# Layer-norm statistics of four token tiles at once, and a first stage that begins with the first four tiles, in an attention and FFN layer on eight cores

## The reference

```python
Q, K, V = x @ wq.T, x @ wk.T, x @ wv.T            # 64 columns each
energy = K.T @ V                                  # 64 x 64, over all tokens
x = layernorm(x + (Q @ energy) * sqrt(3/64) @ wo.T)
h = silu((x @ w1.T) * s1) * ((x @ w2.T) * s2)      # 4096 wide
h = gelu((h @ h1.T) * sh1)                         # 4096 x 4096
h = gelu((h @ h2.T) * sh2)                         # 4096 x 4096
x = layernorm(x + (h @ w3.T) * s3)
```

## Time and profile before

| | us |
|---|---|
| median of 3 runs (lowest, highest) | 2842.74 (2729.49, 3065.65) |
| profiled execution, its own time | 2728.27 |
| its span, slowest core (5) | 2726.4 |
| spans of the eight cores | 2723.3 to 2726.4 |
| TensorE, VectorE, ScalarE busy | 2576.0, 712.3, 342.7 |

### The profile page before, as it was taken

The page is one execution under the profiler, slowest core; times in us unless marked ns, Lnnn a source line. Parts: engine busy times, 40 slices in busy tenths (PEclk is TensorE's granted clock), DMA queues, the critical chain, the costliest instruction groups (busy, mean ns, idle before and its releaser), DMA issues.

```text
span 2726.4 us, 30051 instructions; the slowest of 8 cores (2723.3 to 2726.4 us)
## 1 busy us (share of the span) xinstructions
PE 2576.0 (94%) x12610; PEld 1218.3 (45%) x12610; DVE 712.3 (26%) x771; ACT 342.7 (13%) x429; POOL 0.7 (0%) x7
## 2 busy tenths in 40 slices
PE   4553999999999999999999999999999999999998
PEld 3552444444444444444444444444444444444443
DVE  2335333211111222222224433211111111111124
ACT  1103221100000011111101221100000000000001
POOL 0000000000000000000000000000000000000000
PEclk8665999999999999999999999999999999999999
DMA  9996444444444444544473544444444444444453
GB/s 310 340 342 234 156 155 155 156 152 155 154 155 154 146 163 170 179 162 169 166 266 120 190 155 155 156 153 154 155 154 153 150 149 151 153 155 155 154 185 108
DMA packets 65155, 473.34 MB, mean 174 GB/s; under 512 B 7232, under 2 KB 7360, under 8 KB 15872
## 3 DMA queue, kind: packets, MB, share of 16 engines
q1 hardware_dynamic: 56960, 442.07, 46.5%
q10 hardware_dynamic: 8064, 29.36, 3.2%
HBM read 454.62 MB, written 16.78 MB: 173 GB/s over the span
## 4 chain that ended last, share of the span: by engine, by line
PE 89%; DMA 7%; DVE 2%; ACT 1%; issue 1%; SPq 0%; DVEq 0%; ACTq 0%
PE P L283 65%; PE P L248 16%; DMA HB<-xg 7%; PE P L315 4%; PE P L302 4%; DVE GB L585 1%; DVE GB L531 0%; ACT TS L377 0%; DVE X1B L523 0%; PE P L209 0%; DVE P L546 0%; DVE XZ L549 0%; PE P L216 0%; DVE WR L504 0%; PE P L330 0%
## 5 line engine op out<-in xcount | busy, mean ns | idle before, releaser
L283 PE MATMUL P<-GB,WR 128*128 128x512 bf16 x4096 | 887.1, 379 | 0.0
L283 PE MATMUL P<-HB,WR 128*128 128x512 bf16 x4096 | 884.4, 379 | 0.0
L504 DVE CAST WR<-WST 128x2048 bf16<-128x2048 f32 x328 | 401.6, 1225 | 1405.7 <-PE P L283 1405.7
L283 PEld LDWEIGHTS P<-HB,WR 128*128 128x128 bf16 x4096 | 400.8, 98 | 483.3
L283 PEld LDWEIGHTS P<-GB,WR 128*128 128x128 bf16 x4096 | 399.8, 98 | 482.9 <-issue 3.4
L248 PE MATMUL P<-X1T,WR 128*128 128x512 bf16 x2048 | 444.6, 380 | 0.6 <-DVE HB L559 0.6
L248 PEld LDWEIGHTS P<-X1T,WR 128*128 128x128 bf16 x2048 | 200.8, 98 | 243.8 <-issue 3.8
L330 PE MATMUL P<-GB 128*128 128x128 bf16 x1024 | 99.3, 285 | 101.7 <-DVE GB L585 101.7
L438 ACT ACTIVATE GB<-P,SC 128x1024 bf16<-128x1024 f32 x64 | 71.3, 1115 | 784.8 <-PE P L283 784.8
L559 DVE SCALAR_TENSOR_TENSOR HB<-P,SC,TS 128x512 bf16<-128x512 f32 x128 | 96.0, 751 | 273.8 <-ACT TS L425 273.8
L438 ACT ACTIVATE HB<-P,SC 128x1024 bf16<-128x1024 f32 x64 | 71.3, 1115 | 702.5 <-PE P L283 702.4
(11 more groups left out here) (52 smaller groups left out, 345.6 us busy)
## 6 DMA issues: line engine op xcount, KB each, us to landing
WST<-h SPq DMA_DIRECT2D x256, 1024.0 KB, 4.9
WST<-w SPq DMA_DIRECT2D x96, 1024.0 KB, 5.3
HB<-xg SPq DMA_DIRECT2D x32, 2048.0 KB, 22.3
XZ<-x1s ACTq DMA_DIRECT2D x16, 512.0 KB, 4.1
y<-XZ ACTq DMA_DIRECT2D x16, 512.0 KB, 2.9
GB<-xn SPq DMA_DIRECT2D x8, 512.0 KB, 26.9
x1s<-GB ACTq DMA_DIRECT2D x8, 512.0 KB, 2.8
XZ<-xn ACTq DMA_DIRECT2D x8, 512.0 KB, 6.0
```

The source lines that it names most:

```text
L283: mm = t.matmul(ps[:, g * 512:(g + 1) * 512], W[:, j * 128:(j + 1) * 128], src[:, ic * HALF + g * 512:ic * HALF + g * 512 + 512], start=(i ...
L504: v.tensor_copy(dst, wst(n)).then_inc(s_cast, 1)
```

## The change

- **Last group of x.** Group 31 is loaded by four DMAs of 512 KB, each with a semaphore of its own, and cast in four pieces. TensorE takes two of the eight chunks of E for all four token tiles, as each piece is cast.
- **Statistics.** Tiles 0 to 3, then 4 to 7: VectorE does four adds, and MM, VAR, SD, RS and NMR are made for four columns at once. The add of tile 4 stands between VAR and RS of the first four. The 40 one-column instructions become 10 of four columns.
- **Applies.** The bf16 result goes to GB (x1p), a buffer for each tile. VectorE applies tiles 0 to 2 and 4 to 6, ScalarE tiles 3 and 7 (Identity with scale and bias by token). The transposes go in the order 0, 3, 1, 2, then 4, 7, 5, 6.
- **Stage 1.** Parts 0 to 3 of half 0 use chunks 0 to 3 with tiles 0 to 3, parts 4 to 7 the same chunks with tiles 4 to 7. Part 0 waits for four adds and four copies. The transposes of tiles 4 and 7 stand behind part 2, those of 5 and 6 behind part 3, and part 4 waits for all eight copies. The casts of chunks 3 to 6 are moved to the multiplies of parts 0, 4, 5 and 6.
- **The f32 apply** of the eight tiles is on ScalarE (Identity, in place), behind the Silus of parts 8, 10 to 22, each followed by its store to x1s.
- **SP's order** behind xnat 3: chunk 0, xnat 4, 5, chunk 1, xnat 6, 7, chunk 2.

The diff, cut to its core:

```diff
+FIRST = [(m % 4, m // 4) for m in range(8)]
+TURNS = (0, 3, 1, 2, 4, 7, 5, 6)
...
+    def x1p(t):
+        return GB[:, t * E:(t + 1) * E]
...
+    def stage1_part(h, m):
+        return FIRST[m] if h == 0 and m < 8 else (m // 2, m % 2)
...
             def load_x(g):
                 if g >= 4:
                     s_.wait_ge(s_xc, g - 3)
-                s_.dma_start(out=xst(g), in_=xg[g]).then_inc(s_xl[g % 4], 16)
+                if g < NG - 1:
+                    s_.dma_start(out=xst(g), in_=xg[g]).then_inc(s_xl[g % 4], 16)
+                else:
+                    for i in range(4):
+                        s_.dma_start(out=xst(g)[:, i * 1024:(i + 1) * 1024],
+                                     in_=xg[g][:, i * 1024:(i + 1) * 1024]).then_inc(s_xe[i], 16)
...
@@ -191,12 +209,12 @@
             for t in range(4):
                 load_xnat(t)
             load_chunk(0)
-            load_chunk(1)
             load_xnat(4)
             load_xnat(5)
-            load_chunk(2)
+            load_chunk(1)
             load_xnat(6)
             load_xnat(7)
+            load_chunk(2)
             for n in range(NS, 2 * PER_HALF):
                 load_chunk(n)
...
+            def turn_first(j):
+                k = TURNS[j]
+                if j >= 2:
+                    t.wait_ge(s_te, j - 1)
+                if k % 4 == 3:
+                    t.wait_ge(s_x1c, k // 4 + 1)
+                else:
+                    t.wait_ge(s_x1b, 3 * (k // 4) + k % 4 + 1)
+                for c in range(EC):
+                    tp = t.transpose(pt(j % 2)[:, c * 128:(c + 1) * 128],
+                                     x1p(k)[:, c * 128:(c + 1) * 128], IDB[:])
+                tp.then_inc(s_tp, 1)
...
             def stage1(h):
                 for m in range(64):
-                    oc, g = m // 2, m % 2
+                    oc, g = stage1_part(h, m)
                     M = 64 * h + m
                     n = PER_HALF * h + oc
                     if g == 0:
                         t.wait_ge(s_cast, n + 1)
                     if m >= 3:
                         t.wait_ge(s_hv, M - 2)
-                    elif h == 0:
-                        t.wait_ge(s_sum, 8)
                     else:
-                        t.wait_ge(s_sum, (21, 23, 24)[m])
-                    if m < 2:
-                        t.wait_ge(s_te, 8 * h + 4 * (g + 1))
+                        t.wait_ge(s_sum, ((4, 7, 8), (21, 23, 24))[h][m])
+                    if m == 0:
+                        t.wait_ge(s_te, 4 + 12 * h)
+                    if m == 4 and h == 0:
+                        t.wait_ge(s_te, 8)
                     W = wr(RING_HALF * h + oc)
                     ps = pair(h, m)
                     for w in range(2):
@@ -250,6 +281,9 @@
                                           X1T[:, c * HALF + g * 512:c * HALF + g * 512 + 512],
                                           start=(c == 0), stop=(c == EC - 1))
                     mm.then_inc(s_m1, 1)
+                    if h == 0 and (m == 2 or m == 3):
+                        turn_first(2 * m)
+                        turn_first(2 * m + 1)
...
             t.wait_ge(s_kc, 1)
             for g in range(NG):
-                t.wait_ge(s_xc, g + 1)
                 if g >= 4:
                     t.wait_ge(s_kve, g - 3)
+                if g == NG - 1:
+                    for c in range(EC):
+                        if c % 2 == 0:
+                            t.wait_ge(s_xc, g + c // 2 + 1)
+                        for i in range(4):
+                            mm = t.matmul(kvp(g)[:, i * 128:(i + 1) * 128],
+                                          xbf(g, c * 512 + i * 128, c * 512 + i * 128 + 128),
+                                          KQVB[:, c * 192:c * 192 + 128],
+                                          start=(c == 0 and i == 0),
+                                          stop=(c == EC - 1 and i == 3))
+                    mm.then_inc(s_kvq, 1)
+                    energy(g - 1)
+                    break
+                t.wait_ge(s_xc, g + 1)
                 for i in range(4):
...
             for k in range(3):
                 attn(k, P[k])
-            for k in range(8):
-                if k >= 2:
-                    t.wait_ge(s_te, k - 1)
-                turn(k, k % 2)
-                if k + 3 < 8:
-                    t.wait_ge(s_sum, k + 1)
-                    attn(k + 3, P[(k + 3) % 3])
+            for k in range(3, 6):
+                t.wait_ge(s_sum, k - 2)
+                attn(k, P[k % 3])
+            t.wait_ge(s_sum, 5)
+            attn(6, P[1])
+            for j in range(4):
+                turn_first(j)
+            t.wait_ge(s_sum, 6)
+            attn(7, P[2])
             for h in range(2):
                 stage1(h)
...
+            def root(k, n=1):
+                s.wait_ge(s_var, (k + 4) // 4 if n == 4 else k - 5)
+                s.activation(SD[:, k:k + n], VAR[:, k:k + n], AF.Sqrt, bias=CST[:, 0:1],
                              scale=1.0).then_inc(s_sd, 1)
+
+            def put_first(j):
+                k = TURNS[j]
+                s.wait_ge(s_tp, j + 1)
+                s.copy(X1Tv[:, :, k * 128:(k + 1) * 128],
+                       pt(j % 2).rearrange("p (c t) -> p c t", c=EC)).then_inc(s_te, 1)
+
+            def spill_first(k):
+                s.wait_ge(s_x1b, 6)
+                s.wait_ge(s_x1c, 2)
+                s.activation(xnat(k), xnat(k), AF.Identity, bias=NMR[:, k:k + 1],
+                             scale=RS[:, k:k + 1]).then_inc(s_x1f, 1)
+                s.wait_ge(s_x1f, k + 1)
+                s.dma_start(out=x1s[k * 128:(k + 1) * 128, :], in_=xnat(k)).then_inc(s_xns, 16)
...
             def stage1(h):
                 for m in range(64):
+                    oc, g = stage1_part(h, m)
                     M = 64 * h + m
+                    if h == 0 and (m == 2 or m == 3):
+                        put_first(2 * m)
+                        put_first(2 * m + 1)
                     s.wait_ge(s_m1, M + 1)
                     if M >= 2:
                         s.wait_ge(s_hv, M - 1)
                     s.activation(TS[:, (m % 2) * 512:(m % 2 + 1) * 512], pair(h, m)[:, 0:512],
                                  AF.Silu, bias=0.0,
-                                 scale=SC[:, m // 2:m // 2 + 1]).then_inc(s_sil, 1)
+                                 scale=SC[:, oc:oc + 1]).then_inc(s_sil, 1)
+                    if h == 0 and m >= 8 and m < 24 and m % 2 == 0:
+                        spill_first((m - 8) // 2)
...
+            for gr in range(2):
+                for k in range(4 * gr, 4 * gr + 4):
+                    square(k, xnat(k), x1p(8 + k % 4))
+                root(4 * gr, 4)
+                k = 4 * gr + 3
+                s.wait_ge(s_nmr, gr + 1)
+                s.activation(x1p(k), xnat(k), AF.Identity, bias=NMR[:, k:k + 1],
+                             scale=RS[:, k:k + 1]).then_inc(s_x1c, 1)
+                if gr == 0:
+                    for j in range(4):
+                        put_first(j)
             s.wait_ge(s_scl, 16)
             load_xz(0)
...
-                    if back < 32:
+                    if back < 4 and of == 0:
+                        v.wait_ge(s_m1, back + 5)
+                    elif back < 32:
                         v.wait_ge(s_m1, 64 * of + 2 * back + 2)
...
+            def statistics(k, n):
+                i = k // 4 + 1 if n == 4 else k - 5
+                v.scalar_tensor_tensor(MM[:, k:k + n], NM[:, k:k + n], 1.0 / (E * E),
+                                       NM[:, k:k + n], ALU.mult, ALU.mult).then_inc(s_mm2, 1)
+                v.wait_ge(s_sq, k + n)
+                v.wait_ge(s_mm2, i)
+                v.scalar_tensor_tensor(VAR[:, k:k + n], SSQ[:, k:k + n], 1.0 / E,
+                                       MM[:, k:k + n], ALU.mult,
+                                       ALU.subtract).then_inc(s_var, 1)
+
+            def factors(k, n):
+                i = k // 4 + 1 if n == 4 else k - 5
+                v.wait_ge(s_sd, i)
+                v.reciprocal(RS[:, k:k + n], SD[:, k:k + n]).then_inc(s_rs, 1)
+                v.wait_ge(s_rs, i)
+                v.scalar_tensor_tensor(NMR[:, k:k + n], NM[:, k:k + n], -1.0 / E,
+                                       RS[:, k:k + n], ALU.mult, ALU.mult).then_inc(s_nmr, 1)
+                v.wait_ge(s_nmr, i)
+
+            def apply_first(k):
+                v.tensor_scalar(x1p(k), xnat(k), RS[:, k:k + 1], NMR[:, k:k + 1], ALU.mult,
+                                ALU.add).then_inc(s_x1b, 1)
...
-                    if g == 0:
+                    if h == 0 and m < 8:
+                        if m == 0 or m >= 4 and m < 7:
+                            cast(3 if m == 0 else m)
+                    elif g == 0:
                         cast(PER_HALF * h + oc + 3)
...
+                if g == NG - 1:
+                    for i in range(4):
+                        v.wait_ge(s_xe[i], 16)
```

(68 more changed lines are left out.)

13 lines of the change are left out of this document (removed).

## The result

| us | before | after |
|---|---|---|
| profiled execution, its own time | 2728.27 | 2696.08 |
| its span, slowest core | 2726.4 | 2694.5 |
| spans of the eight cores, median | 2724.1 | 2691.4 |
| median of its first runs (lowest, highest) | 2786.11 (2729.18, 3065.65), 4 runs | 2724.73 (2696.08, 3006.62), 4 runs |
| median in a later job (lowest, highest) | 2729.03 (2728.50, 3139.92), 7 runs | 2695.50 (2694.43, 2950.78), 4 runs |

The ratio is 0.9879, with a 95% interval of 0.9836 to 0.9921; measured again it is 0.9876 (0.9855 to 0.9897). The change gains 1.2%, 32 to 34 us.

A forecast was written before the change was run, and what follows sets the result against it. From 272 us the kernel was taken as one string of TensorE matmuls, so an earlier start shortens it. Gains of 26.3 (early stage 1, net of stalls and transposes) and 3.0 (group 31) make 29.3: 2728.3 to 2699, range 2690 to 2714.

The forecast's parts named there:

- Base: Starting level: the profiled execution, 2728.27 us, the level of the lowest run (2729.49), not of the three runs' median (2842.74).
- Part 2: Statistics of four tiles, first add to stage 1: fewer chains and an early start let stage 1 begin 32.7 us earlier.
- Part 3: Start of stage 1: stalls of 2.7 and 1.7 and four tiles' transposes at 0.5 each shrink the lead to 26.3.
- rival (a): A smoother start: XZ issues take 0.45 both times, clock is up for group 31; gain 33, 2695; chance 0.12.
- Part 1: Group 31 of x in four pieces: its matmuls end earlier, by 2.4 (lower clock) to 4.0 (higher); 3.0 us taken.
- The second stall: Start of stage 1: TensorE's part 4 waits 1.7 us for ScalarE's copies of the last transposes.
- The first, 2.7: Start of stage 1: TensorE's part 3 waits 2.7 us for a multiply and cast 3, behind ScalarE's XZ issues and Silu 0.
- Part 4: The f32 apply and store on ScalarE in stage 1, eight times: covered, costing nothing.
- rival (b): A rougher start: table loads at copies and Identities between Silus, clock falls in the stalls; gain 21 to 25, 2705; chance 0.2.
- (c): The early part hardly pays: a transfer comes 15 us late to add 4 or part 1; gain 5 to 15; chance 0.08.
- (d): Slower: TensorE, fed in bursts, keeps 1.2 GHz in stage 1, a part takes 6.9 for 3.44; 100 us give 2749; chance 0.04.

The follow-up runs named there:

- Experiment 7: The changed kernel with ScalarE held by a copy of 3,600 columns (3.2 us) ahead of its two XZ issues; span 2696.1, ratio to the kernel before 0.9888.

## Why the prediction was right or wrong

**The number.** 2699 forecast, 2696.1 in the profiled execution and 2695.5 measured again: gain 29.3 forecast, 32 to 34 measured. The first runs' median, 2724.73, lies outside 2690 to 2714. The step that failed there is **Base**: I tied the number to the level of the lowest run (2729.49), and neither the sum nor the range has a term for what lifted the old kernel's own median to 2842.74. In its place the four first runs showed 2696.08, 2696.28, 2753.18 and 3006.62, whose median is 28 us above the first two. Measured again, the median is 2695.50, so those 28 us are no cost of the change; what lifts such executions stays open. Against the level that Base names, the sum was 3 to 4 us short of the gain. By the marks: 0.5 and 0.6 more at group 31, 0.7 less in Part 2, 3.0 more in Part 3, so 32.7 for 29.3. What came is nearly rival (a)'s total, gain 33 and 2695, and by its reasons: the short issue, and a clock that is up for group 31. It had a chance of 0.12. The range's low bound, 2690, is 2 us below what its own terms give (2728.3 - 33 - 3).

**Part 1** was 3.0 and is 3.5, with 0.6 more behind it. The backlog behind group 30's energy was there on seven of the eight cores, but the 32 matmuls behind it took 2.0 to 2.9 us where they ran without a hole, so in good part at the higher clock (1.95) and not the lower (3.57). I had leaned to the wrong side. With it that short, the last piece's landing was the bound on seven cores of the first profile and three of the second, 1.7 us ahead of the copy. "The last piece lands at 211.4" was wrong too: it lands 0.3 to 1 us later than one load would. The two errors nearly cancel, and that is luck. The Trainium skill's rule on loads under 1 MiB ("DMA: Bandwidth & Descriptors", Bandwidth) was weighed as worth 2 us and set aside; the four loads of 512 KB did land up to 1 us later, and two of 1 MB did not.

**Part 2** was 32.7 and is 32.0, by the order of steps as written. An add behind an add takes 1.47, not 1.34: the 1.34 is the time from an add to the square that waits for it (219.64 to 220.97 on core 2 again), and the next add starts another 0.15 later, at 221.12, with VectorE idle for 0.24 ahead of it. So the first apply is 9.2 and not 8.8 behind the first add. The inputs were there, as the landings said: in the rows above no add and no apply waits for a DMA.

**Part 3** was a loss of 6.4 and is 2.8 to 3.4. The second stall is 1.72 against 1.7. The first, 2.7, isn't there: its term was an issue of 3.21 carried over from the old trace, and it took 0.39. Experiment 7 put the time back and the stall appeared, in full on three cores. The chain behind it (table load, Silu, multiply, cast 3, part 3) was right; its first link did not belong to the load but to a place in the list. The term had a second flaw: "the first 0.5 us behind the copy" misreads the old trace (core 5):

```profile
270.74 1.01 ACT L387 COPY X1T<-P 128x1024 bf16<-128x1024 bf16 x1 [1.87 <-PE P L216]
...
271.50 3.69 ACTq L402 DMA_DIRECT2D XZ<-xn  x2
```

The issue starts at 271.50, and the copy runs until 271.75. Here too the issues lay beside ScalarE's work. Placed as in the changed kernel (at 241.38, the apply done at 242.55), an issue of 3.21 and one of 0.45 would hold ScalarE for 2.5 us, an estimate from these rows, and not for 4.1. Rival (a) named the short issue; a duration seven times its sibling's, with no reason in the row, deserved more than 0.12. The rest is the clock: part 0 was reckoned at 5.7, and on cores such as core 0, where the clock rose ahead of it, it took 3.5.

**Part 4** was 0 and is 0. Identity took 1.23 and brought no table load; nor did the copies between Silus, so rival (b)'s loads fell. The Trainium skill ("ScalarE: Activation LUTs", Table sets) has copy and identity in every table set. The trace agrees: L443 (Identity) and L437 (copy) have no load among their eight rows each. Rival (b)'s other half, a clock that falls in a stall, didn't occur in the changed kernel with its stall of 1.72 us, but did on all three cores where experiment 7 made one of 3.12. Rivals (c) and (d) did not occur: the granted clock is 1.00 from 255 us on.

## What to carry to other kernels

When small steps go back and forth between two engines, price what the batch no longer stands in front of, too: here the lists behind it gained 5 us beside the 8 of the waits. Early pieces of a load need early casts more than early bytes: casting one landed load in four gave 2.8 of 3.5 us. And before a long duration is carried into a new place, look whether its neighbours of the same kind have it; if not, it may be the place's and not the operation's, as it was here. Last, read a wait on more than the slowest core: core 2 alone said that TensorE had no backlog, and seven others said the opposite.

## What the runs showed of the hardware

- A load's issue on ScalarE's queue lasted 3.2 us on all eight cores and 0.4 when two instructions earlier, with one packet on the instruction queue inside it in the first case.
- A hole of 3.1 us in TensorE was followed by a part at 5.30 in place of 3.4 to 3.6 us on all three cores that had one (experiment 7): it cost about 1.5 times its length. Holes of 1.0 to 1.9 us, on the five other cores there and ahead of part 4 on all eight, left the granted clock at 1.00.
- Split into four loads of 512 KB (rows of 4 KB), 2 MB landed 6.8 to 7.2 us behind the group before, as one load or two 6.2 to 6.5. The four landed unevenly, each 1.0 to 4.1 us behind the load before it. The core's DMA engines moved as much meanwhile: 332 to 345 GB/s from 205 to 212 us with the four (cores 0, 2 and 5), 331 to 342 with the one. So the later landing is not a lower rate; its cause is open.
